# Three PSUM buffers in place of two for the turned chunks of a graph attention kernel

## The reference

```python
h = jnp.maximum(_layernorm(x, axis=-1), 0.0)
proj = jnp.einsum('nf,hfo->hno', h, W)
scores = leaky_relu(s_src[:, :, None] + s_tgt[:, None, :], negative_slope=0.2)
attn = jax.nn.softmax(adj[None, :, :] + scores, axis=1)
vals = jnp.einsum('hij,hjo->hio', attn, proj)
vals = elu(vals + h[None, :, :])
out = x + vals.mean(axis=0)
```

## Time and profile before

| what | us |
|---|---|
| median of 3 executions | 894.86 |
| lowest and highest | 894.77, 895.99 |
| the profiled execution's own time | 894.86 |
| its span in the trace | 893.1 |
| busy: DVE, ACT, PE, POOL | 787.7, 696.2, 691.0, 282.8 |
| last exponential starts | 798.43 |
| last scatter is issued | 803.51 |

### The profile page before, as it was taken

The page is one execution under the profiler, slowest core; times in us unless marked ns, Lnnn a source line. Parts: engine busy times, 40 slices in busy tenths (PEclk is TensorE's granted clock), DMA queues, the critical chain, the costliest instruction groups (busy, mean ns, idle before and its releaser), DMA issues.

```text
span 893.1 us, 15102 instructions
## 1 busy us (share of the span) xinstructions
PE 691.0 (77%) x5026; PEld 560.2 (63%) x5026; DVE 787.7 (88%) x812; ACT 696.2 (78%) x1187; POOL 282.8 (32%) x161
## 2 busy tenths in 40 slices
PE   2405888888878878878888788788788788898995
PEld 1304777766766767767767667667667667764441
DVE  3975999999999999999999999999999998835887
ACT  0594878878868878879779778779788788886885
POOL 1000102232232333324323323422423324234886
PEclk9758899999999999999999999999999999999998
DMA  9999999999999999999999999999999999719713
GB/s 258 335 375 394 373 372 372 371 372 372 371 371 368 374 370 373 370 370 373 370 370 374 367 375 371 371 371 371 371 369 373 371 364 302 180 13 239 200 48 85
DMA packets 223849, 294.43 MB, mean 330 GB/s; under 512 B 4546, under 2 KB 218050, under 8 KB 223812
## 3 DMA queue, kind: packets, MB, share of 16 engines
q1 hardware_dynamic: 214064, 289.49, 94.4%
q0 software_dynamic: 9216, 4.20, 3.9%
q10 hardware_dynamic: 532, 0.27, 0.1%
HBM read 281.28 MB, written 12.65 MB: 329 GB/s over the span
## 4 chain that ended last, share of the span: by engine, by line
DMA 37%; PE 22%; DVE 21%; issue 10%; ACT 7%; SPq 2%; DVEq 0%; ACTq 0%; POOLq 0%
DMA arena<-in_adj 36%; PE ps L495 14%; DVE arena L699 7%; PE ps L463 6%; ACT ps L591 4%; DVE ps L704 4%; DVE arena L691 3%; SPq L383 2%; DVE arena L827 2%; ACT arena L646 1%; DVE arena L744 1%; DMA sums<-arena 1%; PE ps L534 1%; DVE arena L703 1%; PE ps L470 1%
## 5 line engine op out<-in xcount | busy, mean ns | idle before, releaser
L591 ACT ACTIVATE ps<-ps,arena 128x1024 f32<-128x1024 f32 x512 | 555.9, 1086 | 157.5 <-DVE arena L703 86.7
L495 PE MATMUL ps<-ident,arena 128*128 128x128 f32 x4096 | 541.2, 279 | 78.6 <-ACT ps L591 76.4
L495 PEld LDWEIGHTS ps<-ident,arena 128*128 128x128 f32 x4096 | 449.8, 142 | 156.6 <-ACT ps L591 153.0
L674 DVE TENSOR_TENSOR arena<-arena 128x3072 f32<-128x3072 f32 (+2 forms) x115 | 359.3, 3125 | 14.6 <-DMA arena<-in_adj 10.3
L436 POOL DMA_INDIRECT sums<-arena x64 | 179.4, 2803 | 508.4 <-DVE arena L738 210.8
L463 PE MATMUL ps<-ident,arena 128*128 128x128 f32 x512 | 69.8, 280 | 100.1 <-DVE arena L691 76.2
L463 PEld LDWEIGHTS ps<-ident,arena 128*128 128x128 f32 x512 | 57.4, 144 | 110.7 <-issue 68.4
L591 ACT ACTIVATION_READ_ACCUMULATOR ps<-ps,arena 128x1 f32 x512 | 100.3, 196 | 0.0
L699 DVE TENSOR_REDUCE arena<-ps 128x1 f32<-128x1024 f32 x64 | 78.2, 1222 | 15.5 <-PE ps L463 13.4
L691 DVE TENSOR_TENSOR arena<-arena 128x1024 f32<-128x1024 f32 x64 | 76.4, 1221 | 17.1 <-DMA arena<-in_adj 16.9
L704 DVE SCALAR_TENSOR_TENSOR ps<-ps,arena 128x1024 f32<-128x1024 f32 x64 | 82.1, 1282 | 0.0
(11 more groups left out here) (84 smaller groups left out, 225.5 us busy)
## 6 DMA issues: line engine op xcount, KB each, us to landing
arena<-in_adj SPq DMA_DIRECT2D x160, 1536.0 KB, 14.7
arena<-in_adj SPq DMA_DIRECT2D x16, 512.0 KB, 7.3
arena<-in_adj SPq DMA_DIRECT2D x8, 1024.0 KB, 10.5
sums<-arena SPq DMA_DIRECT2D x1, 4160.0 KB, 22.2
out<-arena SPq DMA_DIRECT2D x15, 256.0 KB, 2.6
arena<-sums SPq DMA_DIRECT2D x7, 512.0 KB, 8.0
sums<-arena POOLq DMA_INDIRECT x64, 8.5
arena<-sums SPq DMA_DIRECT2D x2, 256.0 KB, 3.1
```

The costliest lines, as they stand in the source:

```text
L495: mm = pe.transpose(turned_ps[n % 2][:, m, :], piece(g, i, r)[:, m, q * P:(q + 1) * P], ident[:, :])
L591: act.activation(turned_ps[n % 2], turned_ps[n % 2], ACT.Exp, scale=KAPPA, bias=cert[:, i, q, G:G + 1], accum_out=cert[:, i, q, r:r + 1]). ...
L674: dve.tensor_tensor(acc_of(nq), acc_of(nq), piece(g, i, r), ALU.max).then_inc(f_acc, 1)
```

## The change

The turned chunks get three PSUM tensors (0, 1 and 3), so PE may turn chunk n when ACT is done with chunk n - 3. The turned indices and the sums of same rows move into tensor 2, which the turned maxima use. Since they now share banks, two waits are new. Before PE turns indices, all sets of the strip at hand must have gone through line 704 (`f_up`); before it turns the first maxima of a strip, the copy of the sums that lie there must be done (`f_rows`). For strips of two sets and for strip 20 the index, sum and copy steps stand later. The spreading of the attention rows moves from PE's start to after chunk 1 of strip 0. In the tail `open_banks(2)` stands behind the last sum and copy.

```diff
-    turned_ps = [c["psum"][b][:, :].rearrange("p (t i) -> p t i", i=P) for b in range(2)]
+    turned_ps = [c["psum"][b][:, :].rearrange("p (t i) -> p t i", i=P) for b in (0, 1, 3)]
     cells_ps = c["psum"][2]
-    idx_ps = c["psum"][3][:, 0:NQ * P].rearrange("p (q i) -> p q i", i=P)
-    sum_ps = c["psum"][3][:, 512:512 + NQ * F1].rearrange("p (q f) -> p q f", f=F1)
+    idx_ps = c["psum"][2][:, 0:NQ * P].rearrange("p (q i) -> p q i", i=P)
+    sum_ps = c["psum"][2][:, 512:512 + NQ * F1].rearrange("p (q f) -> p q f", f=F1)
...
+    def buffer_of(g, i, n):
+        return ((sets_to(g, i) if known(g) else WIDTHS[0] - NQ) * G + n) % BUFFERS
...
-    IDX_AT = {1: 1, 2: 2, 3: 8}
-    SUM_AT = {1: 2, 2: 4, 3: 13}
-    COPY_AT = {1: 2, 2: 4, 3: 15}
-    SOON = {STRIPS - 3: (6, 9, 10)}
+    IDX_AT = {1: 1, 2: 5, 3: 8}
+    SUM_AT = {1: 2, 2: 7, 3: 13}
+    COPY_AT = {1: 2, 2: 8, 3: 15}
+    SOON = {STRIPS - 3: (8, 10, 11)}
...
-    OPENED = {2: 1, 0: 2, 1: 3}
+    BUFFERS = 3
+    OPENED = {0: 1, 1: 2, 2: 3}
...
+                if q == 0 and known(g) and number(g, i) == 1:
+                    pe.wait_ge(s_set, 2)
+                if q == 0 and (not known(g) or number(g, i) >= 2):
+                    pe.wait_ge(f_rows, number(g, i) - 1)
...
-                    mm = pe.transpose(turned_ps[n % 2][:, m, :], ...
+                    mm = pe.transpose(turned_ps[buffer_of(g, i, n)][:, m, :], ...
...
+                    if first_strip(g, i) and n == 1:
+                        spread_rows()
                     if not first_strip(g, i):
                         if n == index_at(g, i)[0]:
+                            pe.wait_ge(f_up, sets_to(g, i) + nq)
                             turn_idx(*former_of(g, i))
...
-            pe.wait_ge(f_up, NT)
-            open_banks(2)
+            pe.wait_ge(f_exp, NT * G + BUFFERS)
             turn_idx((STRIPS - 1) // BODY, (STRIPS - 1) % BODY)
             sum_same((STRIPS - 1) // BODY, (STRIPS - 1) % BODY)
-
-            pe.wait_ge(f_exp, NT * G + 2)
             open_banks(0)
             open_banks(1)
             pe.wait_ge(f_rows, STRIPS)
+            open_banks(2)
```

More of the change, by code:

```diff
@@ L188, in peaked_path @@
     check_ps = c["psum"][3][:, 512:1024]
-    a_ps = c["psum"][3][:, :].rearrange("p (k h o) -> p k h o", k=2, h=H)
+    a_ps = c["psum"][2][:, :].rearrange("p (k h o) -> p k h o", k=2, h=H)
     s_w = sem("weights_landed")
@@ L427, in former @@
                 if not last_strip(g, i):
-                    pool.wait_ge(f_exp, at(g, i, nq * G) + 2)
+                    pool.wait_ge(f_exp, at(g, i, nq * G) + BUFFERS)
                     pool.tensor_copy(hist[:, bass.ds(sets_to(g, i), nq), :], cert[:, i, 0:nq, :]).then_inc(f_kept, 1)
@@ L494, in turn_chunk @@
                 for m in range(RT):
-                    mm = pe.transpose(turned_ps[n % 2][:, m, :], piece(g, i, r)[:, m, q * P:(q + 1) * P], ident[:, :])
+                    mm = pe.transpose(turned_ps[buffer_of(g, i, n)][:, m, :], piece(g, i, r)[:, m, q * P:(q + 1) * P], ident[:, :])
                 mm.then_inc(f_turn, 1)
@@ L542, in open_banks, with spread_rows @@
                 mm.then_inc(t_open, 1)
+            def spread_rows():
+                pe.wait_ge(f_up, 1)
+                pe.wait_ge(s_a, 32)
+                for k in range(2):
+                    mm = pe.matmul(a_ps[:, k], ones[0:1, :], a_row[0:1, k], start=True, stop=True)
+                mm.then_inc(s_spread, 1)
             pe.wait_ge(s_ones, 1)
[L545 to L548, removed]
             pe.wait_ge(s_ident, 1)
             strips_of(pe, strip)
-            pe.wait_ge(f_up, NT)
-            open_banks(2)
+            pe.wait_ge(f_exp, NT * G + BUFFERS)
             turn_idx((STRIPS - 1) // BODY, (STRIPS - 1) % BODY)
             sum_same((STRIPS - 1) // BODY, (STRIPS - 1) % BODY)
-            pe.wait_ge(f_exp, NT * G + 2)
             open_banks(0)
@@ L590, in strip @@
                     act.wait_ge(f_turn, at(g, i, n) + 1)
-                    act.activation(turned_ps[n % 2], turned_ps[n % 2], ACT.Exp, scale=KAPPA, bias=cert[:, i, q, G:G + 1],
+                    turned = turned_ps[buffer_of(g, i, n)]
+                    act.activation(turned, turned, ACT.Exp, scale=KAPPA, bias=cert[:, i, q, G:G + 1],
                                    accum_out=cert[:, i, q, r:r + 1]).then_inc(f_exp, 1)
@@ L610, in copy_sum @@
                 act.wait_ge(f_sum, number(g, i) + 1)
+                if first_strip(g, i):
+                    act.wait_ge(s_cleared, 16)
                 added_before(act, g, i)
@@ L629, in _ @@
             act.dma_start(w_sb[:, :, :], W.rearrange("h f o -> f h o")).then_inc(s_w, 16)
-            act.sem_inc(f_exp, 2)
+            act.sem_inc(f_exp, BUFFERS)
             act.wait_ge(s_const, 1)
@@ L709, in find_rows @@
                 nq, Q = subs(g, i), number(g, i)
-                dve.wait_ge(f_exp, at(g, i, nq * G) + 2)
+                dve.wait_ge(f_exp, at(g, i, nq * G) + BUFFERS)
                 dve.scalar_tensor_tensor(junk[:, 0:nq, :], cert[:, i, 0:nq, 0:G], 0.5,
@@ L804, in strip @@
                     piece_max(*after, 2)
-                if soon or nq == 2:
+                if (soon or nq == 2) and not first_strip(g, i):
                     find_target(*before)
```

## The result

The changed kernel takes 897.78 us (median of 8 runs, 896.66 to 899.11), the kernel before 894.84 us on the same chip (8 runs, 894.47 to 895.99). The ratio is 1.0033, with a 95% interval of 1.0023 to 1.0043: 2.9 us slower, where 0.8 us less was forecast. The profiled execution has a span of 896.1 us, against 893.1.

A forecast was written before the change was run, and what follows sets the result against it. Transfers (371 GB/s) bound the long stage, a chain over ACT, PE and DVE the end. 0 for the long stage, -0.6 at strip 22's maxima, -0.2 behind, 0 in the tail: 894.86 - 0.8 = 894.1 us; range 892.6 to 896.9.

The forecast's parts named there:

- rival 3: Before strip 22's maxima: PE pauses some 3 us and its clock halves, 9 us at most, 903 us; chance 0.02.
- Third buffer: Turned chunks: a pair falls from 2.39 to 2.22 us at ACT's 1.11 us steps; costed at nothing under the transfers.
- rival 2: The whole loop gets faster if DMA's busy share hid a lack of free slots: 856 to 893 us; chance 0.04.
- Strip 20 and 21, the deciding step: Strip 21's copy, four chunks later, holds DVE's find_target: strip 22's maxima turned at 784.88, not 785.49.
- 2.6 us were gained and 0.6 stay: Strip 21's first exponential comes 2.6 us earlier; 0.6 us of that remains at strip 22's maxima.
- break-even: Start of the copy of strip 20's sums, within strip 21, at 777.8 us; each microsecond beyond it costs one.
- Rival 1: ACT and PE keep 1.195 us steps, strip 20's copy at 780.9, strip 22's maxima 3.1 us late: 898.0 us; chance 0.14.
- Bank 2 opened late: Tail: check's first product about 805.9, transposes about 807.1, covered by the sums' load; without cover up to 0.3 us lost.
- Spread rows: Strip 0: rows move behind DVE's first cells, done near 28.7 us, reader starts at 38.62; costed at nothing.
- waits before the maxima: In the loop the copy follows chunk 15 and the next maxima come after chunk 23; costed at nothing.

The follow-up runs named there:

- e4: The changed kernel with the tail's projections in tensors 0, 1, 3 and tensor 3 opened in PE's wait for the last indices: 896.95 us, ratio 1.0025.
- e5: e4 plus 20 unused PE transposes ahead of the wait for a strip's first maxima, from strip 2 on except strip 21: 893.83 us, ratio 0.9991.
- e7: The changed kernel with 20 unused PE transposes ahead of the first maxima of strips 20 and 22 only: 896.01 us, ratio 1.0014.
- e1: The changed kernel with three buffers, but PE turns chunk n only when chunk n - 2 has been exponentiated: 900.45 us, ratio 1.0061.
- e2: The kernel before, two buffers, with only the later index, sum and copy steps of the change: 898.68 us, ratio 1.0037.
- e6: e5 with index, sum and copy steps earlier, after chunks 4, 5, 6 in strip 21 and 7, 9, 10 in strip 20: 891.99 us, ratio 0.9969.
- e9: e6 with 8 extra transposes in place of 20 ahead of the first maxima of strip 22: 891.84 us, ratio 0.9967.
- e8: The kernel before with 8 extra PE transposes ahead of the wait for a strip's first maxima: 895.84 us, ratio 1.0016.

## Why the prediction was wrong

**The step that failed** is the full clock that the sum assumes throughout, with rival 3, "PE's clock falls", set aside at a chance of 0.02. As reason against it I gave that PE is idle for 108 of 620 us, in pauses in every strip, at a granted clock of 1.00. That was a sum of pauses. A single pause before maxima was 1.4 us on the mean; the change makes it 3.6 us, and the longest such pause of the loop before was 2.5 us. I also placed this rival only before strip 22, although the same lead lets PE run dry before every strip. Its price was set the other way, 9 us at most, where it was about 3: e4 and e5, which differ in the extra transposes alone, have ratios of 1.0025 and 0.9991, 0.34% or 3.0 us.

**What the missing 3.8 us are.** The span should have been 892.3 us and is 896.1. Against the forecast, the maxima of strip 22 start 1.25 us late (786.13 for 784.88). In this lie DVE's 0.6 us at 732.79 (from the fall at strip 19's start, see e7) and the half clock after strip 20's pause. The half clock then stretches these maxima and chunk 14, whose exponential is 2.65 us late (789.45 for 786.8). The scatter at 796.85 is 2.6 us late, since strip 22's first exponentials win a little back. In the tail the sums are turned at 812.82, 3.9 us after the forecast's 808.9: 1.3 us more go there, as twelve matmul records take 6.69 us and not 5.4.

**Third buffer.** Right. ACT's step is 1.09 us in long runs, where I took 1.11. The page "ScalarE: Activation LUTs" of the Trainium skill, section "What ACT_TABLE_LOAD costs", gave an estimate of 1.04 us a step; the trace doesn't agree, with 1.09 us. The loop gained nothing from it, at the same 371 GB/s, so rival 2 is out.

**Strip 20 and 21, the deciding step.** Right, and the best test of it is e5: the times fit to 0.3 us. DVE waits 2.22 us for the copy in the change (I had said about 2), and ACT idles 4.96 us before chunk 14 where I had 3.7 us without the clock. "2.6 us were gained and 0.6 stay" holds: e5's maxima of strip 22 are 0.9 us earlier than before. The break-even picture holds too: in e1 and e2 the copy starts 2.25 and 3.2 us beyond 777.8, and the maxima of strip 22 come 2.2 and 3.1 us later than before.

**Rival 1, the copy too late.** It gave 898.0 us, close to the 897.8 us measured, but not by its mechanism. ACT didn't keep the old pace, and the copy started at 778.49, 0.7 us beyond the break-even, 1.3 us later than forecast because the work before it was late. A total that fits a rival's price would have misled here; the rows of maxima at 1.84 and 1.97 us tell the two apart.

**Bank 2 opened late.** Half right. I had found its cover, the load of the sums, to be just enough and its loss at most 0.3 us. e1 has the same order at full clock in its tail: 6.4 us from the last scatter (806.69) to the turned sums (813.10), against 6.2 before, so the loss is 0.2 us. My 807.1 for the 15 transposes was too early for a check's product at 805.9: between the two stand 1.5 us in e1's trace. At the half clock the late bank cost 1.6 us (7.8 us against 6.2). Opening the bank in the pause took that away, and by e1 most of it through the clock.

**Spread rows, waits before the maxima.** Nothing in the result points to them; no kernel tried them alone.

## What to carry to other kernels

In this kernel a deeper buffer let PE run ahead, and what it had run ahead it then waited in one piece. So on PE, look for the longest pause that the change makes in front of work that others wait for, and price that work at half the clock; the share of idle time says nothing about it. In the stage bound by transfers the third buffer gave nothing (371 GB/s with either), and steps placed by count (after chunk n) have to be set anew. An engine that waits for each transfer has a cover of just that wait: DVE had 0.77 us before strip 20, and 1.3 us of lateness went through it. Here the same three buffers were 2.9 us slower as changed, and 2.8 to 3.1 us faster than before (e6, e9) with the pause filled, the bank opened in a wait and the steps of strip 21 one or two chunks earlier.

## What the runs showed of the hardware

- The clock goes with how PE's pauses lie, and not with their sum. From 112 to 732 us PE waited 59.8 us for ACT before chunks and 25.9 us before the first maxima of strips (1.4 us on the mean, 2.5 at most), and the granted clock was 1.00 throughout. After the change it waited 19.4 and 65.2 us (3.2 to 5.2 us a strip), and the clock fell at 15 of 18 strips. PE's busy time rose from 512 to 526 us with no more work, since its matmuls took longer at the lower clock. The page "TensorE: Matmul & The Clock Gate" of the Trainium skill, section "A second HAM failure mode: psum-queue depth-cycling", describes a clock that oscillates when PE idles briefly between groups as it cycles through PSUM, for bf16 matmuls of 512 columns. These traces show the opposite case: the short pauses of the two buffers (0.2 to 0.4 us, every second chunk) went with the full clock, and taking them away brought the oscillation.
- The length of one pause doesn't settle whether the clock falls. Before the maxima at 251.62 us the kernel before pauses 2.53 us and keeps the full clock; e1 and e2 pause 2.51 and 2.50 us before strip 22 and lose it, e1 only behind the maxima. In the change pauses of 3.33, 3.32 and 3.21 us (before 217.22, 562.00 and 664.33 us) were not followed by a fall, and in e1 one of 1.76 us (before 389.38 us) was.
- The spread of a kernel's runs is no sign of such falls: e8 has none in its trace, every one of its runs has a mean clock of 0.969 to 0.971, and its runs lie up to 2.7 us apart.
- ACT's exponentials keep their step of 1.09 us when they come back to back, while the recorded duration grows from 1.08 to 1.20 us within a run of them. So the busy time of ACT rose (560.1 us for 555.9) with no more work.
